# Block SiLU from ScalarE's own table against SiLU built from an exponential on three engines

## What is computed

```python
xn = _layernorm(x)
x = x + _L0_attn_ref(xn, ...) + _L0_ffn_ref(xn, ...)

# _L0_attn_ref: group norm, 16 retention heads, then its own FFN, "the block FFN"
xn = channel_group_norm(x, ffn_norm_g, ffn_norm_b, H)
h = jax.nn.silu(xn @ w1.T + b1)          # 128 -> 256 features
x = residual + (h @ w2.T + b2)           # 256 -> 128

# _L0_ffn_ref: two layers of local attention (8 heads, window 64), each with
h = a * jax.nn.gelu(g, approximate=False)
```

## Time and profile before

| what | before |
|---|---|
| timed runs | 970.54, 972.21, 973.97 us; median 972.21 |
| span of the profiled execution | 969.5 us |
| median less that span | 2.7 us |
| PE busy | 862.3 us, 89% |
| PE weight loads busy | 580.5 us, 60% |
| DVE busy | 634.5 us, 65% |
| ACT busy | 701.7 us, 72% |
| POOL busy | 631.0 us, 65% |
| mean granted TensorE clock | 0.983 of full |
| ACT table loads at L493 | 39, of 1283 ns each |
| one layer-1 body with a block tile | 48.3 us |

### The profile page before, as it was taken

How to read it: one execution, slowest core, us unless ns; L and a number is a source line. 1 busy time by engine, 2 the same in 40 slices (tenths; PEclk the granted TensorE clock), 3 DMA queues, 4 the chain that set the end, 5 groups by cost and what they waited for, 6 DMA issues and landing times.

```text
span 969.5 us, 26414 instructions
## 1 busy us (share of the span) xinstructions
PE 862.3 (89%) x10836; PEld 580.5 (60%) x10836; DVE 634.5 (65%) x1082; ACT 701.7 (72%) x1449; POOL 631.0 (65%) x500
## 2 busy tenths in 40 slices
PE   0678889989899898998999989999999999999876
PEld 0345666666667666666566656565656565656552
DVE  5874666666667567576575776757575758575632
ACT  0446786977868779677797778787878787878651
POOL 4588677675876758667586665757575758585700
PEclk9979999999999999999999999999999999999997
DMA  9100000000000000000000000000000000000000
GB/s 295 30 1 3 1 2 2 3 3 2 2 3 1 3 1 1 3 2 3 1 2 3 1 2 2 1 21 4 17 7 23 2 23 2 21 3 24 1 23 11
DMA packets 20482, 13.47 MB, mean 14 GB/s; under 512 B 4579, under 2 KB 19597, under 8 KB 20237
## 3 DMA queue, kind: packets, MB, share of 16 engines
q1 hardware_dynamic: 15108, 10.49, 3.6%
q10 hardware_dynamic: 5256, 1.31, 0.7%
HBM read 9.70 MB, written 2.10 MB: 12 GB/s over the span
## 4 chain that ended last, share of the span: by engine, by line
PE 63%; ACT 15%; DVE 10%; issue 7%; POOL 3%; DMA 1%; DVEq 0%; POOLq 0%; SPq 0%; ACTq 0%
PE pQK L1181 8%; PE pS L1108 6%; PE pT L1093 5%; PE pT L1050 5%; PE pM L1125 5%; PE pV L1146 4%; PE pS L1082 4%; PE pM L1254 4%; DVE m L734 4%; PE pT L1237 3%; PE pQK L1345 3%; PE pM L1119 2%; PE pS L1069 2%; ACT prT L545 2%; ACT pr L598 1%
## 5 line engine op out<-in xcount | busy, mean ns | idle before, releaser
L366 POOL TENSOR_TENSOR rn<-rn,half_neg 128x16 f32<-128x16 f32 x64 | 187.5, 2929 | 5.3
L379 POOL TENSOR_TENSOR m<-m 128x1024 f32<-128x1024 f32 x64 | 150.9, 2358 | 0.0
L364 POOL TENSOR_SCALAR rn<-ss 128x16 f32<-128x16 f32 x64 | 16.3, 254 | 193.3 <-DVE ss L747 192.1
L386 POOL TENSOR_TENSOR qkn<-m,rn 128x1024 f32<-128x1024 f32 x64 | 121.7, 1902 | 5.0
L1181 PE MATMUL pQK<-wqkv,hT 128*128 128x512 f32 x256 | 123.6, 606 | 0.9 <-DVE m L734 0.9
L780 DVE TENSOR_REDUCE mx<-pS 128x8 f32<-128x1024 f32 x64 | 78.1, 1220 | 63.8 <-PE pS L1082 63.8
L561 ACT ACTIVATE sq<-pQK 128x1024 f32<-128x1024 f32 x64 | 65.4, 1022 | 25.5 <-PE pQK L1181 25.4
L747 DVE TENSOR_REDUCE ss<-sq 128x16 f32<-128x1024 f32 x64 | 77.6, 1213 | 6.7 <-ACT sq L561 6.4
L782 DVE TENSOR_TENSOR pr<-pS,mx 128x1024 f32<-128x1024 f32 x64 | 78.4, 1225 | 2.2
L521 ACT ACTIVATE kT<-pT 128x512 f32<-128x512 f32 x64 | 38.0, 595 | 57.3 <-PE pT L1050 56.8
L545 ACT ACTIVATE prT<-pT 128x1024 f32<-128x1024 f32 x64 | 65.0, 1016 | 15.6 <-PE pT L1093 14.8
(11 more groups left out here) (169 smaller groups left out, 2015.9 us busy)
## 6 DMA issues: line engine op xcount, KB each, us to landing
x<-in_L_attn_x SPq DMA_DIRECT2D x4, 512.0 KB, 9.4
xs<-in_L_attn_x SPq DMA_DIRECT2D x8, 256.0 KB, 2.8
out<-aqkT SPq DMA_DIRECT2D x8, 256.0 KB, 2.2
wqkv<-in_L_ffn_wqkv SPq DMA_DIRECT2D x2, 768.0 KB, 9.8
tab<-in_k_tab SPq DMA_DIRECT2D x1, 1024.0 KB, 10.4
w<-in_L_ffn_w SPq DMA_DIRECT2D x2, 341.0 KB, 10.5
wo<-in_L_ffn_wo SPq DMA_DIRECT2D x2, 256.0 KB
cst<-in_k_cst ACTq DMA_DIRECT2D x1, 404.5 KB, 4.3
```

The source lines that it names most:

```text
L366: eng.tensor_tensor(rn[:, k % 2, :], rn[:, k % 2, :], half_neg[:, 0:2 * H], ALU.pow).then_inc(S["rn_done"], 1)
L379: eng.tensor_tensor(m1[:, k % 2, :], m1[:, k % 2, :], m2[:, :], ALU.add).then_inc(S["add_done"], 1)
L386: eng.tensor_tensor(qkn[:, k % 2, :].rearrange("p (h d) -> p h d", d=DH), m1[:, k % 2, :].rearrange("p (h d) -> p h d", d=DH), rn[:, k % 2 ...
```

## The change

SiLU(z) = z / (1 + exp(-z)) is formed in five steps, each on two halves of 128 x 512, in place of one ScalarE operation on each half:

1. DVE, slot 1, ahead of `dve_scores`: afh = pQK + bias (`dve_block_linear`).
2. ACT, end of slot 1: gg = exp(-afh) (`act_block_decay`).
3. POOL, start of slot 2, ahead of `pool_norm`: gg = gg + 1.
4. DVE, end of slot 2, ahead of slot 3's `dve_scores`: gg = 1 / gg (`dve_block_inverse`).
5. POOL, end of slot 2: afh = afh * gg, which now signals `G["silu"]`.

The q/k projection of slot 1 waits on `G["linear"]` (step 1). ACT no longer loads the Silu table: behind the Gelus of slot 0 it loads Exp at once, and the Exp load of slot 1 is gone. Gelu in slot 0 of the next body waits on `G["silu"]`, because it writes gg again.

```diff
@@ pool_slot
+            block = block_tile(ff) if k == 2 else None
+            if block is not None:
+                for j in range(2):
+                    eng.wait_ge(G["decayed"], 2 * block + j + 1)
+                    eng.tensor_scalar(gg[:, j, :], gg[:, j, :], 1.0, 1.0, ALU.add, ALU.mult).then_inc(G["floor"], 1)
             if new:
                 n = count(new, k)
                 pool_norm(eng, n, k)
                 pool_add(eng, n, k)
                 pool_scale(eng, n, k)
+            if block is not None:
+                for j in range(2):
+                    eng.wait_ge(G["inverse"], 2 * block + j + 1)
+                    eng.tensor_tensor(afh[:, j, :], afh[:, j, :], gg[:, j, :], ALU.mult).then_inc(G["silu"], 1)
@@ act_slot
-            if k == 1 and block_tile(ff) is not None:
-                act_block_ffn(eng, block_tile(ff))
-                act_load_table(eng, ACT.Exp)
...
                 act_load_table(eng, ACT.Gelu)
+                if ff[0] == 1:
+                    eng.wait_ge(G["silu"], 2 * ff[1] + 2)
                 act_gelu(eng, ff, 0)
...
+                if ff and old:
+                    act_load_table(eng, ACT.Exp)
                 if block_tile(ff) is not None:
-                    act_load_table(eng, ACT.Silu)
                     act_block_in(eng, block_tile(ff))
-                elif ff and old:
-                    act_load_table(eng, ACT.Exp)
...
                 if k > 0 and turned:
                     act_exp(eng, b, m)
+            if k == 1 and block_tile(ff) is not None:
+                act_block_decay(eng, ff, block_tile(ff))
...
-        def act_block_ffn(eng, t):
+        def act_block_decay(eng, step, t):
+
+            eng.wait_ge(LS["hf_done"], NC * step_count(step) + NC)
             for j in range(2):
-                eng.wait_ge(G["w1_mm"], 2 * t + j + 1)
-                eng.activation(afh[:, j, :], pQK[:, j * 512:(j + 1) * 512], ACT.Silu, bias=c("b1a", j)).then_inc(G["silu"], 1)
+                eng.wait_ge(G["linear"], 2 * t + j + 1)
+                eng.activation(gg[:, j, :], afh[:, j, :], ACT.Exp, scale=-1.0).then_inc(G["decayed"], 1)
@@ dve_slot
+            block = block_tile(ff)
+            if k == 1 and block is not None:
+                dve_block_linear(eng, block)
             turned = at(new, old, k - 2)
             if turned:
                 dve_scores(eng, turned[1], turned[2])
...
+            if k == 2 and block is not None:
+                dve_block_inverse(eng, block)
...
+        def dve_block_linear(eng, t):
+
+            for j in range(2):
+                eng.wait_ge(G["w1_mm"], 2 * t + j + 1)
+                eng.tensor_scalar(afh[:, j, :], pQK[:, j * 512:(j + 1) * 512], c("b1a", j), None,
+                                  ALU.add).then_inc(G["linear"], 1)
+
+        def dve_block_inverse(eng, t):
+            for j in range(2):
+                eng.wait_ge(G["floor"], 2 * t + j + 1)
+                eng.reciprocal(gg[:, j, :], gg[:, j, :]).then_inc(G["inverse"], 1)
@@ pe_slot
                 if block is not None:
-                    eng.wait_ge(G["silu"], 2 * block + 2)
+                    eng.wait_ge(G["linear"], 2 * block + 2)
```

More of the change, by code:

```diff
@@ L246, in program @@
             "kv_mm", "kvm", "y_mm", "yt", "faded", "state", "ow_mm", "x1", "cs")}
-        G = {n: sem(f"g_{n}") for n in ("xa", "w1_mm", "silu", "blend", "fin_mm", "xs", "osb", "out")}
+        G = {n: sem(f"g_{n}") for n in ("xa", "w1_mm", "linear", "decayed", "floor", "inverse", "silu", "blend", "fin_mm", "xs", "osb", "out")}
         x_steps = a["L0_attn_x"].rearrange("b (t p) d -> t p b d", p=P)
@@ L490, in act_load_table @@
         def act_load_table(eng, function):
-            place = (ACT.Gelu, ACT.Silu, ACT.Exp).index(function)
+            place = (ACT.Gelu, ACT.Exp).index(function)
             eng.activation(warm[:, place:place + 1], half_neg[:, 0:1], function)
```

## The result

| | before | after |
|---|---|---|
| median of the timed runs, us | 972.0 (970.54 to 973.97, 4 runs) | 1012.05 (1010.17 to 1015.93, 4 runs) |
| ratio, 95% interval | 1 | 1.0417 [1.0398, 1.0436] |
| span of the profiled execution, us | 969.5 | 1011.1 |
| mean granted clock | 0.983 | 0.962 |
| a body with a block tile, us | 48.33 | 53.46 to 53.87 |

The account below looks back on a forecast made before the run. PE was taken as nearly the bound, with DVE's reciprocals deciding the change. Span 969.5 + 32.2 for reciprocals net of cover and gain + 7 for PE's clock + 2.7 from span to median gave 1011 us, range 992 to 1036.

Parts of the forecast that it names:

- the removal gives back, per body: Slot 1, without Silu and its table load: PE's 0.69 us wait for oT plus 0.27 us late weights, 0.96 us.
- one reciprocal: DVE, end of slot 2: 128 x 512 reciprocal at 3.2 us, with 0.7 and 3.5 as ends.
- idle time that covers the pair: DVE's 1.34 us wait before xr of slot 3, all the cover there for the two reciprocals.
- net of the reciprocals, per body: 6.4 us of reciprocals less 1.34 idle and 0.96 from slot 1: 4.1 us later per body.
- last body: Two reciprocals stand before 2.89 us idle and nothing was gained: 6.4 - 2.89 = 3.5 us.
- PE's clock, per body: After PE's roughly 5 us gap in slot 3, half clock costs 1 us per body, between nothing and 2.5.
- bias add, exponentials, POOL's steps: DVE's adds, ACT's pair in slot 1 and POOL's steps in slot 2 fit idle time, costing nothing at 3.2 us reciprocals.
- a sign that the prediction had named for being wrong: Prediction is wrong if the chain does not come through xr of slot 3, or the reciprocal lasts under 1.2 us.
- (a): Reciprocal above 3.5 us, or clock falling in each body for 2 us or more: 1031 or 1022 us; chance 0.22.
- (b): Wide reciprocal on DVE streams at about 0.7 us, inside its cover: 965.5, or up to 971 us; chance 0.12.
- (c): VectorE and GpSimd shut each other out, holding reciprocals 3.6 us per body: 1036, or near 991 us; chance 0.10.
- (d): The divide costs about 2.5 us and the clock stays, 2.7 us per body: 993 us; chance 0.06.

Follow-up runs that it names:

- removal and bias add alone: Changed kernel cut to the removed Silu and table loads plus VectorE's bias add, W2 getting z itself: 965.80 us, 0.9944 of the kernel before.
- body without reciprocals: Changed kernel without its two VectorE reciprocals, GpSimd's product following its own addition: 966.80 us, 0.9962 of the kernel before, body 47.39 us.
- three widths: Changed kernel with reciprocals over 128 or 256 of the 512 columns: 967.46 and 978.98 us; the whole 512 took 1012.05 us.
- hole filled: Whole change plus five unread TensorE products in slot 3 of the seven bodies, before the values: 1006.81 us, 1.0372 of the kernel before.
- the version with tanh: Changed kernel with ScalarE's tanh for the exponential, POOL's addition also halving, no reciprocal, whole SiLU computed: 968.07 us, 0.9953 of the kernel before.

## Why the prediction was right

The forecast was 1011 us, and the median is 1012.05. Its terms:

| step of the sum | predicted | measured | where |
|---|---|---|---|
| the removal gives back, per body | 0.96 us | 0.96 (removal and bias add alone); 0.94 (body without reciprocals); 0.95 (kT of slot 1 to xr of slot 1: 9.25 before, 8.30 after) | timelines |
| one reciprocal | 3.2 us | 3.32 | shape row |
| idle time that covers the pair | 1.34 us | 1.34 in the kernel without it, 1.54 from the bodies of three widths | timelines |
| net of the reciprocals, per body | 4.1 us | 52.40 - 48.33 = 4.07 | hole filled |
| last body | 3.5 us | 3.4 | tail |
| PE's clock, per body | 1 us, bounds 0 and 2.5 | 1.16 | hole filled |
| body | 53.4 us | 53.46 to 53.87 | |
| bias add, exponentials, POOL's steps | nothing | 0.02 us per body | removal alone |

The removal. PE's timeline after has the output projection of slot 1 at 1.05 us with no wait for ACT's oT in front of it, where 0.69 stood:

```profile
651.45 1.05 PE L1153 MATMUL pM<-oT,wo 128*128 128x128 f32 x8
```

That it was worth its full bound, and no other wait was as late, is what the two kernels without reciprocals show.

The reciprocal's price was the step that could have failed, since no row showed a wide one. It was put together from small rows: the excess of an 8-element reciprocal over an 8-element copy, read as a cost per element. The three wide ones bear that reading out, at 6.25 ns within the 5.2 to 6.5 that those rows gave, and 0.12 us fixed where 0.15 was taken; the copy's own rate of 1.05 ns was not measured apart. With the pair at 6.55 us for 6.4 and the cover at 1.54 for 1.34, two small errors cancel in the net. By the Trainium skill (VectorE: DVE Perf Modes, the part on the fixed hardware budget), the estimate from a repeat count of 8 was 8.3 ns and 4.4 us. The trace has 6.25 ns and 3.32 us; the measurement decides.

The place of the delay held too. The maximum of slot 3 comes 6.46 us later behind xr of slot 2 (10.90 against 4.44), less the 0.95 of slot 1: 5.5 us later in the body, as said. The idle time before xr is gone. From there on the prediction's chain went through xr and the layer norm; behind the hole the chain of the changed kernel takes the other branch that was named, the subtraction and `pe_values`. Half clock is not the reason: with the hole filled and the clock at 1.00 the chain takes it too, and goes from the values through DVE's output scaling to the statistics:

```profile
672.58 1.17 PE pS L1136 x32
...
674.71 0.81 DVE lbst L872 x4
```

So a sign that the prediction had named for being wrong did come: xr of slot 3 is not what the chain comes through. The price is the same, since xr stands directly behind that subtraction in the same queue: from xr to xr the slot is 13.24 - 8.25 = 4.99 us longer, and the body 5.01 with the clock up. From xr of slot 3 to the layer norm's apply it is 6.89 us, where it was 5.82: that 1.07 is the clock's price once more, seen in the slot where it is paid (with the hole filled it is 5.83).

The last body. DVE's timeline of it, against the earlier trace rows:

```profile
979.32 6.55 DVE L866 RECIPROCAL gg<-gg 128x512 f32<-128x512 f32 x2
985.79 0.23 DVE L813 TENSOR_TENSOR xr<-pM,x2T 128x128 f32<-128x128 f32 x1
```

The 2.89 us of idle time are gone; the rest of the pair, 6.55 - 2.89 = 3.66 us, is near the 3.4 by which the tail is longer.

POOL. An addition took 621 ns (0.8 assumed) and a product 1263 (1.18 assumed); 3.77 us in all, of the 4.04 that were free. Nothing was late in the changed kernel, where DVE is later anyway; in the version with tanh it shows that this fitted by only 0.23 us. This was the thinnest cover in the sum.

The sizes that were off are small: the bodies cost 37.0 us, clock alike near 910 us, where 35.7 were summed, and the tail 3.4 for 3.5. Three differences that the sum did not hold are no effects of its terms: 2.9 us more ahead of the tiles, 1.7 less for the fall of the clock near 910 us that only before had, and 0.95 us from span to median where 2.7 were taken. They cancel to within 0.6 us. So the mechanism and its sizes were right to about 1.3 us in 37, but that the forecast came within 1 us of the median is luck in part.

The rivals. (a) Heavier: out, with the reciprocal below 3.5 us and the clock below 2. (b) The reciprocal streams: out; with an operation that does stream the time was 968.4, inside its 965.5 to 971. (c) The lock: POOL's add and scale took 2.35 and 1.90 us in the body above, while the reciprocals ran, as in rows of before, and the pair took 6.47 us in the chain for two of 3.2: neither engine held the other. (d) Lighter: out, with 3.32 us for a reciprocal, 4.07 net per body where it had 2.7, and a clock that fell. POOL's rows for (c), beside the reciprocals from 665.69 us:

```profile
666.23 2.35 POOL L388 TENSOR_TENSOR m<-m 128x1024 f32<-128x1024 f32 x1
668.66 1.90 POOL L395 TENSOR_TENSOR qkn<-m,rn 128x1024 f32<-128x1024 f32 x1
```

## What to carry to other kernels

An operation that the trace shows only small could be priced here by its excess over a copy of the same size, element by element; that the excess grows with the width was a choice, which the runs at three widths then bore out. What it then costs is its length less the idle time in its own slot, not in its engine's total (DVE was idle for a third of the span). A hole on TensorE can cost twice, once for its length and once for the clock behind it: here in all seven bodies with the whole reciprocal, and in four of them with half of it. And before an inverse is put on VectorE, look for a form without one: the tanh form kept the gain of the single table set and cost no reciprocal.

## What had not been expected of the hardware

- The wide reciprocal costs 6.25 ns per element: 917, 1718 and 3318 ns for 128, 256 and 512, where `tensor_scalar` on the same 512 elements took 419 ns.
- Idle time on PE is not free for what follows: five matmuls per body that nobody reads, put into the hole, kept the clock at 1.00 and took 8.1 us off the seven bodies.
- The same wait lowers the clock in one execution and not in the next. PE stands 2.67 us ahead of the projection of v near 560 us in the version with tanh and in the one without reciprocals; in the first the granted clock then fell to 0.50, in the second it stayed at 1.00. PE's rows there, one from each kernel:

```profile
561.46 1.52 PE L1172 MATMUL pV<-wqkv,hT 128*128 128x512 f32 x2 [2.67 <-DVE gst L975]
```

```profile
558.98 1.10 PE L1172 MATMUL pV<-wqkv,hT 128*128 128x512 f32 x2 [2.67 <-DVE gst L975]
```

What decides between the two isn't settled. The thin stretch near 910 us is of the same kind, at 1.7 us. Where a kernel sits at such an edge, its time moves by about 2 us from run to run, and a body's period tells more than a median of a few runs.
